# Cross-attention in two phases with all scores in SBUF, on one core of a Trainium2 chip

## The reference

```python
scores = jnp.einsum('bqd,bkd->bqk', query, value)
distribution = jax.nn.softmax(scores, axis=-1)
attention = jnp.einsum('bqk,bkd->bqd', distribution, value)
...
bias = jnp.where(causal, slopes * rel, -jnp.inf)
...
x = x + _L0_xattn_ref(_layernorm(x, axis=-1), ctx_1024)
x = x + _L0_attn_ref(_layernorm(x, axis=-1), L0_attn_w_attn, L0_attn_w_proj)
x = x + _L0_ffn_ref(_layernorm(x, axis=-1), L0_ffn_Wg, L0_ffn_W1, L0_ffn_W2, L0_ffn_W3)
```

## Time and profile before

| | |
|---|---|
| time, median of 3 runs | 133.56 us (132.82 to 136.61) |
| span of the profiled execution | 134.4 us |
| busy: PE, PEld | 117.0 us (87%), 87.9 us (65%) |
| busy: DVE, ACT, POOL | 96.3 us (72%), 68.1 us (51%), 56.5 us (42%) |
| chain that ended last | DVE 45%, PE 30%, ACT 10%, issue 8% |

### The profile page before, as it was taken

How to read it: one execution, slowest core, us unless ns; L and a number is a source line. 1 busy time by engine, 2 the same in 40 slices (tenths; PEclk the granted TensorE clock), 3 DMA queues, 4 the chain that set the end, 5 groups by cost and what they waited for, 6 DMA issues and landing times.

```text
span 134.4 us, 2666 instructions
## 1 busy us (share of the span) xinstructions
PE 117.0 (87%) x838; PEld 87.9 (65%) x838; DVE 96.3 (72%) x260; ACT 68.1 (51%) x171; POOL 56.5 (42%) x56
## 2 busy tenths in 40 slices
PE   5990599998989898998896999998999898799982
PEld 5770489896969697887794956554467577534540
DVE  0899566798988979798958887998867489410312
ACT  3470745866757483938421439989690320415100
POOL 2599075292948577585501799500000330300000
PEclk9999779999999999999999999999999999999999
DMA  4998878879999100059000000000057989300002
GB/s 133 356 369 251 273 274 294 258 226 304 429 441 468 68 0 0 0 156 454 22 0 0 2 0 0 0 5 2 0 141 322 458 351 444 166 0 0 0 5 78
DMA packets 3754, 22.69 MB, mean 169 GB/s; under 512 B 544, under 2 KB 800, under 8 KB 3232
## 3 DMA queue, kind: packets, MB, share of 16 engines
q1 hardware_dynamic: 3744, 22.55, 44.6%
HBM read 22.29 MB, written 0.26 MB: 168 GB/s over the span
## 4 chain that ended last, share of the span: by engine, by line
DVE 45%; PE 30%; ACT 10%; issue 8%; DMA 2%; POOL 2%; ACTq 1%; DVEq 1%
DVE denom L485 7%; DVE wup_sb L448 7%; PE bank L1047 5%; DVE negmax L471 5%; DVE chunkneg L468 3%; ACT p_hi L707 3%; PE bank L918 3%; PE bank L1062 3%; DVE v_sb L552 3%; DVE wup_sb L563 2%; ACT v_sb L768 2%; PE bank L948 2%; DVE acc L490 2%; DMA x_sb<-x_in 2%; PE bank L965 2%
## 5 line engine op out<-in xcount | busy, mean ns | idle before, releaser
L365 POOL TENSOR_TENSOR k_lo<-wdn_sb,k_hi (+1 forms) x7 | 16.9, 2414 | 16.1 <-ACT k_hi L677 16.0
L369 POOL TENSOR_TENSOR v_lo<-v_sb,v_hi (+1 forms) x8 | 19.5, 2441 | 4.1 <-ACT v_hi L682 4.1
L696 ACT ACTIVATE wup_sb<-bank,negmax 128x512 f32<-128x512 f32 x16 | 11.0, 687 | 16.7 <-DVE negmax L471 11.7
L866 PE MATMUL bank<-v_hi,p_hi 128*128 128x256 f32 (+1 forms) x64 | 19.4, 303 | 0.0
L867 PE MATMUL bank<-v_lo,p_hi 128*128 128x256 f32 (+1 forms) x64 | 18.0, 282 | 0.0
L868 PE MATMUL bank<-v_hi,p_lo 128*128 128x256 f32 (+1 forms) x64 | 18.0, 282 | 0.0
L855 PE MATMUL bank<-ident,wup_sb 128*128 128x128 f32 x64 | 10.5, 289 | 7.6 <-ACT wup_sb L696 7.6
L332 POOL TENSOR_TENSOR rstd<-vareps,power 128x1 f32<-128x1 f32 x6 | 3.4, 573 | 29.7 <-DVE vareps L422 29.6
L855 PEld LDWEIGHTS bank<-ident,wup_sb 128*128 128x128 f32 x64 | 7.6, 146 | 12.0 <-ACT wup_sb L696 10.9
L457 DVE TENSOR_TENSOR p_lo<-bank,p_hi 128x512 fp32r<-128x512 f32 x16 | 11.0, 686 | 6.3 <-ACT p_hi L707 6.3
L768 ACT ACTIVATE v_sb<-wup_sb,nmax 128x128 f32<-128x128 f32 (+1 forms) x32 | 14.1, 443 | 2.2 <-DVE nmax L563 2.2
(11 more groups left out here) (120 smaller groups left out, 236.9 us busy)
## 6 DMA issues: line engine op xcount, KB each, us to landing
wup_sb<-w_up SPq DMA_DIRECT2D x2, 4096.0 KB, 14.6
wdn_sb<-ctx_t SPq DMA_DIRECT2D x8, 512.0 KB, 4.1
v_sb<-ctx_v SPq DMA_DIRECT2D x8, 512.0 KB, 4.5
wdn_sb<-w_down SPq DMA_DIRECT2D x2, 2048.0 KB, 10.6
wqkv_sb<-w_qkv SPq DMA_DIRECT2D x1, 768.0 KB, 7.2
x_sb<-x_in SPq DMA_DIRECT2D x1, 256.0 KB, 2.8
wproj_sb<-w_proj SPq DMA_DIRECT2D x1, 256.0 KB, 7.3
x_out_dram<-v_sb SPq DMA_DIRECT2D x2, 128.0 KB, 1.8
```

The source lines that it names most:

```text
L365: nc.gpsimd.tensor_tensor(k_lo[:, i % 2], kT[:, i], k_hi[:, i % 2].bitcast(FP32), ALU.subtract).then_inc(k_lo_ready, 1)
L369: nc.gpsimd.tensor_tensor(v_lo[:, i % 2], v_sb[:, i], v_hi[:, i % 2].bitcast(FP32), ALU.subtract).then_inc(v_lo_ready, 1)
L866: nc.tensor.matmul(o_bank[b][:, 0:C], p_hi[:, b, n], v_hi[:, i % 2, n], start=(n == 0), stop=False)
```

## The change

Cross-attention becomes two phases. In the first, TensorE makes the scores of all sixteen tiles, ScalarE copies each from PSUM to `scores_sb` in SBUF (`keep_scores`), and VectorE takes each tile's maximum from there (`chunk_max`). Once all of a block are in, one `row_max` gives the final maximum. In the second, ScalarE takes the exponential in place, and transposes, splits and value matmuls run tile by tile; outputs gather in PSUM over all chunks, and the row sum with them, from a column of ones in `v_hi`. So the shrinking, `denom` and `acc` go. The tiles' orders are two tables, of which the diff shows the lines.

Who splits what moves too: ScalarE makes `k_hi`, GpSimd `k_lo` of chunks 2 to 7 and then `v_hi` as a cast, VectorE `k_lo` of 0 and 1 and all `v_lo`. Keys load into three buffers and values into two. All 16 heads of bias are made in phase 1, four after each of the first four chunks. Three dummy matmuls before the second norm go. The names of regions change; `mask_k`, `bias_unit` and all that follows stay as they were, and the expert weights `wdn` and the second half of `wup` are loaded after the phases, both before the self-attention ends.

```diff
+S_TILES = [(i, b) for i in range(NCH - 2) for b in range(TB)] + [(i, b) for b in range(TB) for i in (NCH - 2, NCH - 1)]
+P_TILES = [(0, 0), (1, 0)] + [t for i in range(2, NCH) for t in ((i, 0), (i - 2, 1))] + [(NCH - 2, 1), (NCH - 1, 1)]
+S_AT = {t: n for n, t in enumerate(S_TILES)}
+P_AT = {t: n for n, t in enumerate(P_TILES)}
+SB, PB, KB, VB = 4, 3, 3, 4
...
+            for i in range(KB):
+                sync.dma_start(k_in[:, i], ctx_t[i]).then_inc(k_loaded[i], 16)
+            for i in range(2):
+                sync.dma_start(v_in[:, i], ctx_v[i]).then_inc(v_loaded[i], 16)
+            for i in range(KB, NCH):
+
+                sync.wait_ge(k_lo_ready, i - KB + 1)
...
+            for i in range(2, NCH):
+
+                sync.wait_ge(v_lo_ready, i - 1)
+                sync.dma_start(v_in[:, i % 2], ctx_v[i]).then_inc(v_loaded[i % 2], 16)
...
+            def split_k_lo(i):
+
+                pool.wait_ge(k_lo_ready, i)
+                pool.wait_ge(k_hi_ready, i + 1)
+                nc.gpsimd.tensor_tensor(k_lo[:, i % KB], k_in[:, i % KB], k_hi[:, i % KB].bitcast(FP32),
+                                        ALU.subtract).then_inc(k_lo_ready, 1)
+
+            def split_v_hi(i):
+                pool.wait_ge(v_loaded[i % 2], 16 * (i // 2 + 1))
+                if i >= VB:
+
+                    pool.wait_ge(values_ready, P_AT[i - VB, 1] + 1)
+                nc.gpsimd.tensor_copy(v_hi[:, i % VB, :, 0:C], v_in[:, i % 2]).then_inc(v_hi_ready, 1)
+
+            for i in range(2, NCH):
+                split_k_lo(i)
+            for i in range(NCH):
+                split_v_hi(i)
+
...
+            def split_v_lo(i):
+
+                dve.wait_ge(v_hi_ready, i + 1)
+                nc.vector.tensor_tensor(v_lo[:, i % VB], v_in[:, i % 2], v_hi[:, i % VB, :, 0:C].bitcast(FP32),
+                                        ALU.subtract).then_inc(v_lo_ready, 1)
+
+            def chunk_max(i, b):
+                n = S_AT[i, b]
+                dve.wait_ge(scores_kept_s, n + 1)
+                nc.vector.tensor_reduce(chunkneg[:, b, i:i + 1], scores_sb[:, b, i], AX.X, ALU.max,
+                                        negate=True).then_inc(chunkmax_ready, 1)
...
+            split_k_lo(1)
...
+            for i in range(NCH - 2):
+                for b in range(TB):
+                    chunk_max(i, b)
+                if i < 4:
+                    bias_heads(4 * i, 4 * i + 4)
+            chunk_max(NCH - 2, 0)
+            split_v_lo(0)
+            chunk_max(NCH - 1, 0)
+            row_max(0)
+            chunk_max(NCH - 2, 1)
+            split_v_lo(1)
+            chunk_max(NCH - 1, 1)
+            row_max(1)
+            lo_of(*P_TILES[0])
+            for h in range(1, TB * NCH):
+                if h % 2 and (h + 3) // 2 < NCH:
+                    split_v_lo((h + 3) // 2)
+                lo_of(*P_TILES[h])
+                if P_TILES[h] == (NCH - 2, 1):
+                    add_attention(0)
+                    norm_stats(0)
             norm_apply(1, 0)
             add_attention(1)
...
+            def keep_scores(i, b):
+                n = S_AT[i, b]
+                scalar.wait_ge(scores_in_psum, n + 1)
+                nc.scalar.activation(scores_sb[:, b, i], s_bank[n % SB][:, :], ACT.Copy).then_inc(scores_kept_s, 1)
+
+            def exps(i, b):
+
+                scalar.wait_ge(negmax_ready, b + 1)
+                scalar.wait_ge(scores_kept_s, S_AT[i, b] + 1)
+                nc.scalar.activation(scores_sb[:, b, i], scores_sb[:, b, i], ACT.Exp,
+                                     bias=negmax[:, b:b + 1]).then_inc(probs_ready, 1)
...
+            for i in range(NCH - 2):
+                split_k_hi(i + 2)
+                for b in range(TB):
+                    keep_scores(i, b)
+            keep_scores(NCH - 2, 0)
+            keep_scores(NCH - 1, 0)
+            exps(*P_TILES[0])
+            exps(*P_TILES[1])
+            keep_scores(NCH - 2, 1)
+            exps(*P_TILES[2])
+            hi_of(*P_TILES[0])
+            keep_scores(NCH - 1, 1)
+            for h in range(1, TB * NCH):
+                if h + 2 < TB * NCH:
+                    exps(*P_TILES[h + 2])
+                hi_of(*P_TILES[h])
 
...
+            def room_for_scores(i, b):
+                n = S_AT[i, b]
+                pe.wait_ge(k_lo_ready, i + 1)
+                if n >= SB:
+                    pe.wait_ge(scores_kept_s, n - SB + 1)
...
+            def values_of(i, b):
+                h = P_AT[i, b]
+                pe.wait_ge(p_lo_ready, h + 1)
+                pe.wait_ge(v_lo_ready, i + 1)
+                hi, lo = o_bank[b][:, 0:C + 2], o_bank[b][:, 0:C]
+                for n in range(NT):
+                    nc.tensor.matmul(hi, p_hi[:, h % PB, n], v_hi[:, i % VB, n], start=(i == 0 and n == 0), stop=False)
+                    nc.tensor.matmul(lo, p_hi[:, h % PB, n], v_lo[:, i % VB, n], start=False, stop=False)
+                    last = nc.tensor.matmul(hi, p_lo[:, h % PB, n], v_hi[:, i % VB, n], start=False,
+                                            stop=(i == NCH - 1 and n == NT - 1))
+                last.then_inc(values_ready, 1)
...
+            room_for_scores(*S_TILES[-1])
+            scores_half(*S_TILES[-1], 0)
+            transpose_of(*P_TILES[0])
+            scores_half(*S_TILES[-1], 1)
+            pe.wait_ge(v_ones_ready, 2)
+            transpose_of(*P_TILES[1])
+
+            pe.wait_ge(scores_kept_s, TB * NCH - 3)
+            transpose_of(*P_TILES[2])
+            for h in range(TB * NCH):
+                values_of(*P_TILES[h])
+                if h + PB < TB * NCH:
+                    transpose_of(*P_TILES[h + PB])
+                if h == TB * NCH - 2:
+                    norm_T(1, 0)
...
-            keep_warm(banks[0], WARM_BEFORE_NORM_1)
...
-            bias_heads(MORE_BIASES, LATE_BIASES)
```

More of the change, by code:

```diff
@@ L115, in build @@
-        k_lo = sb("k_lo", [P, 2, KC, CH], FP32R)
-        v_hi = sb("v_hi", [P, 2, NT, C], FP32R)
-        v_lo = sb("v_lo", [P, 2, NT, C], FP32R)
-        p_hi = sb("p_hi", [P, TB, NT, P], FP32R)
-        p_lo = sb("p_lo", [P, TB, NT, P], FP32R)
-        before_up = [wup_sb[:, 4:8].rearrange("p e w k h -> p (e w k h)"), 0]
-        before_dn = [wdn_sb[:, 4:8].rearrange("p e k c -> p (e k c)"), 0]
-        over_v = [v_sb[:, :, :, :].rearrange("p i n c -> p (i n c)"), 0]
-        bias = carve(before_up, NH * 3 * P, "p (h k) -> p h k", h=NH)
@@ new lines, in build @@
+        wup_lo = at("wup_lo", [P, 4, 2, KC, H], up_first)
+        up_last = region(4 * 2 * KC * H)
+        wup_hi = at("wup_hi", [P, 4, 2, KC, H], up_last)
+        scores_sb = at("scores_sb", [P, TB, NCH, CH], up_last)
+        wup_of = [wup_lo, wup_hi]
+        down = region(E * KH * C)
+        wdn_sb = at("wdn_sb", [P, E, KH, C], down)
+        k_hi = at("k_hi", [P, KB, KC, CH], down, FP32R)
+        k_lo = at("k_lo", [P, KB, KC, CH], down + KB * KC * CH * 4, FP32R)
+        v_in = at("v_in", [P, 2, NT, C], down + 2 * KB * KC * CH * 4)
@@ new lines, in build, with carve @@
+        room = region(KB * KC * CH)
+        k_in = at("k_in", [P, KB, KC, CH], room)
+        p_hi = at("p_hi", [P, PB, NT, P], room, FP32R)
+        p_lo = at("p_lo", [P, PB, NT, P], room + PB * CH * 4, FP32R)
+        split_probs = room
+        room = region(VB * NT * (2 * C + 2))
+        v_hi = at("v_hi", [P, VB, NT, C + 2], room, FP32R)
+        v_lo = at("v_lo", [P, VB, NT, C], room + VB * NT * (C + 2) * 4, FP32R)
+        over_v_first = room
+        over_v = [over_v_first]
+        def carve(name, shape, region_at):
+            first = region_at[0]
+            region_at[0] += (math.prod(shape[1:]) * 4 + 63) // 64 * 64
+            return at(name, shape, first)
@@ L443, in _, with split_k_lo @@
                                         ALU.subtract).then_inc(q_lo_ready, 1)
+            def split_k_lo(i):
+                dve.wait_ge(k_hi_ready, i + 1)
+                nc.vector.tensor_tensor(k_lo[:, i % KB], k_in[:, i % KB], k_hi[:, i % KB].bitcast(FP32),
+                                        ALU.subtract).then_inc(k_lo_ready, 1)
             def bias_heads(first, end):
                 for h in range(first, end):
[L448 removed]
@@ new lines, in lo_of, with add_attention @@
+            def lo_of(i, b):
+                h = P_AT[i, b]
+                dve.wait_ge(p_hi_ready, h + 1)
+                nc.vector.tensor_tensor(p_lo[:, h % PB].rearrange("p n q -> p (n q)"), t_bank[h % PB][:, :],
+                                        p_hi[:, h % PB].rearrange("p n q -> p (n q)").bitcast(FP32),
+                                        ALU.subtract).then_inc(p_lo_ready, 1)
+            def add_attention(b):
+                dve.wait_ge(values_ready, P_AT[NCH - 1, b] + 1)
+                step(nc.vector.reciprocal(rdenom[:, b:b + 1], o_bank[b][:, C:C + 1]))
+                step(nc.vector.scalar_tensor_tensor(x_sb[:, b], o_bank[b][:, 0:C], rdenom[:, b:b + 1], x_sb[:, b],
```

(10 more changed lines are left out.)

390 lines of the change are left out of this document (106 added, 284 removed).

## The result

The changed kernel takes 139.45 us (median; 138.03 to 142.69) against 134.06 for the kernel before on the same chip. The ratio is 1.039, with a 95% interval of 1.029 to 1.050: slower, near the forecast of 138.8. The profiled execution of the changed kernel took 140.03 us, its span is 138.0, 3.6 more than the profiled one of before.

A forecast was written before the change was run, and what follows sets the result against it. VectorE, its SBUF instructions waiting for whole GpSimd subtracts, was taken to hold the cross-attention loop. Span 134.4 + 5.9 (end of values) + 1.8 (clock) - 2.5 (seam) = 139.6, less 0.8 to the median: 138.8 us, range 131 to 146.

The forecast's parts named there:

- Blocked heads: Phase 1, VectorE: bias heads wait for whole GpSimd subtracts, one passing at each end; cost 6.2 us, row maximum at 37.5.
- The maxima don't wait: Phase 1: VectorE's maxima from SBUF don't wait for GpSimd's subtracts; five microseconds, due if they did, stay out.
- The ring: Phase 2: value matmuls, cast, `v_lo` and `p_lo` wait on each other; 5.0 us per two tiles, four rounds 20.0.
- The clock: First value tiles: after TensorE idles from 29.8 to 42.8, about 4 us of half clock cost 1.8 us (0 to 3).
- 0.65 or less about 43 us: Sign to look for: TensorE's granted clock this low around the first values, forecast at 42.8 us.
- The end of the values: Phase 2: last values end at 76.9 us against 70.95 before, adding 5.9; the clock's 1.8 is a separate term.
- The seam: Last value matmul to first biased unit and after: multiply-add, transpose, mask and last heads save together 2.5 us.
- From span to median: Last step: the sum of 139.6 us is taken 0.8 lower, as before's median was below its span, giving 138.8 us.
- Heads that get through: Rival, phase 1: heads pass GpSimd's subtracts, row maximum at 31.3; 132.7 us (130 to 135); chance 0.25.
- this rival's point on chunk 2: With heads unblocked, `v_in` of chunk 2 stands behind 5 MB of weights, lands near 34; values end near 71.5.
- TensorE as the pace: Rival: TensorE sets the pace all through, values from 35, sixteen tiles of 1.86 to 65; 125 us; chance 0.07.
- the third: Rival: GpSimd's cast is as slow as its subtract, or the maxima wait too; 144 to 147 us; chance 0.13.

## Why the prediction was right, and where not

**Blocked heads: right.** Forecast: the second group passes one head for each seam, row maximum at 37.5, 6.2 us late. Measured 36.0 and 35.4; the kernels without the wait have it at 29.4 to 31.0, so the price is 5 to 6.6 us. It was 1.5 sooner than forecast for two reasons: heads 8 to 11 were through at 29.0, where the forecast's are at 29.9, and VectorE's free work from there on took 7.1 us for 7.6.

**The maxima don't wait: right.** From SBUF, under a running subtract, two take 1.28 us (14.04), as they did from PSUM. The Trainium skill, "SBUF — State Buffer", Who interferes with whom, has it so for `tensor_reduce`; the trace agrees, with 0.68 us for one.

**The ring: right, 5.0 forecast, 4.79 measured.** The mis-sized term is the cast: 1.3 forecast, 1.05 measured. The lower bound, from the memset (0.95), was nearer than half a subtract. The Trainium skill, "GPSIMD Engine Reference", 3.1 Elementwise, puts the body at 1.03 cycles an element where at most two operations are done; at the engine's 1.2 GHz that is an estimate of 0.88 us for the body of 1024 elements. The trace shows 1.05 us for the whole cast; no run here takes body and rest apart.

**The clock: the mechanism right, the size not a number.** 1.8 us forecast for the first values. In the profiled execution TensorE's hole was 5.5 us; the granted clock was 0.65 from 36.9 to 41.5, under the pieces ahead of the values, and whole from the first value on. In the second the hole was 6.9 us and the clock 0.50 from 36.3 to 44.9. The fourth tile ended 7.3 and 9.1 us after the first began, so the cost was 0 and 1.8 us. The sign "0.65 or less about 43 us" showed in the second alone.

**The end of the values: 3.8 too late in the sum** (78.7 with the clock, 74.9 measured): 1.1 of it was there at the end of the fourth tile (48.9 for 50.0), 0.8 are four rounds of 4.79 for 5.0, and the clock's 1.8 didn't come. In the second profiled execution it came, and they end at 76.1.

**The seam: 2.5 forecast, 2.1 measured.** 1.5 between the values and the first biased unit, where 1.9 was forecast, and 0.6 behind it, as forecast.

**The experts: nothing forecast, +1.7.** The step that failed is one that wasn't made: I took all behind the seam as it was, though the granted clock there isn't a property of the code alone.

**From span to median: wrong, and lucky.** I took the median as 0.8 below the span, because before's median lay 0.8 below the span that I read. But that span belonged to the slowest of its three times, and a time is longer than its span in every execution (2.0 us in the changed kernel's: 140.03 against 138.0). The end of the values was worked out from nothing and had no share in that slowness, so a span of 139.6 means 141.6 us, 2.8 above the forecast of 138.8. That forecast came within 0.7 of the median of 139.45 because the span itself was forecast 1.6 too long: 3.8 at the values, less 0.4 at the seam and 1.7 at the experts. So the forecast is right in what waits for what, and its last digit is luck. What the slip hides: against before the change costs 5.3 us by the medians, not the 3.6 between the two profiles, because before lost 2.4 us more at its start in the very execution I read.

**Rivals.** Heads that get through: excluded by the rows. But this rival's point on chunk 2 held: with the heads gone, its load, and the slow clock behind that wait, take 4.7 of the 6.9 us gained. TensorE as the pace: true once heads, ring and weights are out of the way, and then the kernel runs at 127 to 128 us. The casts at 1.05 us exclude the third.

## To carry to other kernels

In these kernels a plain `tensor_scalar` in SBUF cost next to nothing by its own size beside a GpSimd that subtracts in SBUF back to back: it cost a whole subtract for each 0.3 us or so of such work, and everything behind it in VectorE's order paid. Place such work where GpSimd rests, or try a slower form that doesn't wait. Where an instruction waits for a buffer that a later one frees, look at what stands behind it in order; one place later was worth 4 us here. And before a wait at the start is priced from one profile, a second profile of the same kernel is worth having: two of before differed by 2.4 us of span, with 0.3 us of phase between two engines at the start.
